# Layer 1's gate scores computed on VectorE in place of TensorE

## The chip, the cores and the metric

The kernel runs on one core of a Trainium2 chip. The metric is the device time of one execution in microseconds (us). Engines are named as in the profile: PE or TensorE (matmuls), PEld (its weight loads), DVE or VectorE, ACT or ScalarE, POOL or GpSimd, SP or SyncE, which here only issues DMAs.

## The reference

Two layers of a graph network with a gated mixture of experts behind each run on 3125 rows of 256 f32 values. The part that matters is the end of layer 1:

```python
x = x + gnn1(layernorm(x), edges)              # two mean-aggregating convolutions
n = layernorm(x)
gates = softmax(n @ gW + gb)                   # gW: 256 x 4, one column per expert
topv, topi = top_k(gates, 2)
topw = softmax(topv)
x = x + shared_mlp(n) + sum_k topw[k] * expert[topi[k]](n)
```

The change touches only how n @ gW + gb, four scores per row, is computed. Layer 0 has a gate too (8 experts); it goes through the same code with routing set and stays as it is.

## The kernel before, in words

Rows lie in 25 tiles (TILES) of 128 partitions. The function second_conv (L1780) is the second convolution of a layer, its layer norm, and the gate's scores. For layer 1 it is called with final set and routing unset; its tiles carry the tag l1b_.

TensorE first multiplies 25 dense tiles and beside them sums the neighbours of tiles 0 to 9 (early, L2284). Then one_tile (L2299) sums one tile after another, 10 to 24, with 49 matmuls each. For the work behind it, the tiles stand in seven groups, SIZES = (4, 4, 4, 4, 4, 3, 2). The table BETWEEN says at which half of which tile TensorE breaks off for a group:

```python
BETWEEN = {(12, 0): [("turn", 0)], (12, 1): [("score", 0)], (13, 0): [("back", 0)], ...
           (15, 1): [("turn", 2)], ... (18, 1): [("turn", 3)], ... (21, 1): [("turn", 4)], ...
           (24, 0): [("turn", 5), ...], (24, 1): [("score", 5), ("back", 5), ..., ("turn", 6), ...
```

- turn (L2310) waits until all tiles of the group are normalised (norm_done) and transposes them to PSUM. ScalarE copies them to SBUF (take_turned, L2207) and stores them for the final stage (xt_out).
- score (L2322) multiplies the gate's weights, padded to strips of 32 columns, with each turned tile, half of the 256 features at a time (the trace has two matmul records for each, since the data are f32). ScalarE copies the four strips (take_flat, L2219).
- back (L2335) turns the strips back into rows. VectorE adds the gate's bias and writes last_scores (take_scores, L2069).
- head: the first eight products of the final stage's experts (L1692), which run behind turns and scores of groups 5 and 6; ScalarE takes them (L1702).

VectorE works through one queue in this order: finish(0), part of finish(1) and (2), then for each group c take_scores(c) and finish(c + 2). finish adds the bias to the raw rows (L2021), adds each tile's sum from PSUM (L2027), takes the statistics (L170 to L185, with a root by ScalarE at L219) and normalises (L2045). Before it normalises over the raw rows, it waits until ScalarE's queue has stored them (x_out, L2194).

TensorE waits for VectorE in turn, and in one_tile where a bank of sums is opened again (sum_done). SyncE loads raw rows of groups 3, 4 and 5 into the place of groups 0, 1 and 2 once those are turned (load_rows, L1895), then the early weights of the final stage (final.load, L1726). The gate's weights and bias are loaded at the sixth dense tile (L1910, L1911).

The final stage, last_experts (L2981), starts when all engines have left second_conv. VectorE computes the softmax, the two largest and their weights from last_scores (from L3233); TensorE does expert products beside it, and then needs those weights for its own transposes (L3161).

Of the kernel before, what the change touches and what calls it, by code (L numbers as in the profile page):

```python
# [12 lines left out]
F32, F16, BF16, I32 = mybir.dt.float32, mybir.dt.float16, mybir.dt.bfloat16, mybir.dt.int32  # L13
ALU = mybir.AluOpType
# [4 lines left out]
P = 128  # L19
D = 256  # L20
KD = D // P
# [1714 lines left out]
SIZES = (4, 4, 4, 4, 4, 3, 2)  # L1736
STARTS = tuple(sum(SIZES[:c]) for c in range(len(SIZES) + 1))
# [3 lines left out]
STRIP = 32  # L1741
# [38 lines left out]
def second_conv(nc, io, g, adj, parts, tag, names, gate, rows_from, rows_to, work, sums_of, routing=None, final=None):  # L1780
# [4 lines left out]
    with ExitStack() as ctx:  # L1785
        pr = Prog(nc, ctx, tag, g["used_sems"])
# [3 lines left out]
        held = work.held + [third[:, :]]  # L1790
# [14 lines left out]
        normed = lambda c: labelled(c)[:, :, 0:D]  # L1805
        AFTER = {3: 0, 4: 1, 5: 2}
# [4 lines left out]
        E = gate_w.shape[1]  # L1811
        if routing:
# [14 lines left out]
            first_tile = {"xt": pr.sb("expert_xt", [P, KD, ST], F32), "xr": pr.sb("expert_xr", [P, ST // P, DW], F32),  # L1827
                          "ids_now": row_i[:, 0:2 * (ST // P)].rearrange("p (a t) -> p a t", a=2)}
            weights = expert_weights(parts, pr.sb("expert_w1", [P, KD, H0], F32), pr.sb("expert_b1", [P, 2, HB], F32))
        wg = pr.sb("gate_w", [P, KD, E], F32)  # L1830
        strips_of_wg = held[1][:, 0:KD * STRIP].rearrange("p (k e) -> p k e", k=KD)
        bg = pr.sb("gate_b", [P, E], F32)
        st = pr.sb("st", [P, CT, 6], F32)
        mv = pr.sb("mv", [P, CT, 2], F32)
# [43 lines left out]
        @block.sync  # L1878
        def _(sp):
            def load(k):  # L1880
                r = k % RING
                if k >= RING:
                    sp.wait_ge(s["dense_done"], k - RING + 1)
                for sem, count in sums_of(k):
                    sp.wait_ge(g[sem], count)
                work.load_sums(sp, k, s[f"in{r}"])
                work.load_inverse(sp, k, s[f"in{r}"])

            def load_x(k):
                if k >= XB:  # L1890
                    sp.wait_ge(s[f"pre_out{k % XB}"], 16 * (k // XB))
                sp.dma_start(xb(k), tile_of(rows_from, k)).then_inc(s[f"x_in{k % XB}"], 16)

            def load_rows(c):
                sp.dma_start(rows_of(c), chunk_of(g["pre"], c)).then_inc(s[f"rows_in{c}"], 16)  # L1895

            for u in range(XB - 1):
                sp.sem_inc(s[f"x_in{u}"], 16)
            load(LOADED)
            load_x(XB - 1)  # L1900
            for k in range(LOADED + 1, RING):
                load(k)

            def load_vectors(k):

                if k == 4:
                    sp.dma_start(by_row[:, :], g["inv"].rearrange("a (t p) -> (a p) t", p=P), allow_slow_non_contiguous=True
                                 ).then_inc(s["by_row_in"], 16)
                elif k == 5:
                    sp.dma_start(wg[:, :, :], gate_w.rearrange("(k p) e -> p k e", p=P)).then_inc(s["gate_in"], 16)  # L1910
                    sp.dma_start(bg[:, :], gate_b.rearrange("(a e) -> a e", a=1).broadcast_to([P, E])).then_inc(s["gate_in"], 16)  # L1911
                elif k == 7:
                    sp.dma_start(bias[:, :], io[b].rearrange("(a n) -> a n", a=1).broadcast_to([P, D])).then_inc(s["bias_in"], 16)

            for k in range(TILES):
                if k + RING < TILES:
                    load(k + RING)
                if 1 <= k and k + XB - 1 < TILES:
                    load_x(k + XB - 1)
                load_vectors(k)  # L1920
                if k == MOST + 2:
                    for u in range(XB):
                        sp.wait_ge(s[f"pre_out{u}"], 16 * len(range(u, MOST, XB)))
                    load_rows(0)
            for u in range(XB):
                sp.wait_ge(s[f"pre_out{u}"], 16 * uses(u))
            sp.wait_ge(s["dense_done"], TILES)
            load_rows(1)
            sp.wait_ge(s["x_out"], 16)
            for c in (2, 6):  # L1930
                load_rows(c)
            for c in (3, 4, 5):
                if routing:
                    sp.wait_ge(s[f"scattered{AFTER[c]}"], 16 * 2 * SIZES[AFTER[c]])
                sp.wait_ge(s["turned"], AFTER[c] + 1)
                load_rows(c)
            if final:


                sp.wait_ge(s["agg_done"], EARLY_TILES)  # L1940
                final.load(sp, s["final_in"])
                sp.wait_ge(s["xt_out"], 16 * 2)
                final.load_rows(sp, 0, s["final_in"])
                sp.wait_ge(s["final_in"], 16 * (final.FIRST + final.SECOND + 1))
            if routing:
                follow["sync_early"](sp)
                sp.wait_ge(s["agg_done"], TILES)
                follow["sync"](sp)
# [53 lines left out]
        def _(dve):  # L2002
# [62 lines left out]
                normalise(1)  # L2065

            def take_scores(c):
                dve.wait_ge(s["scored"], c + 1)
                nc.vector.tensor_tensor(g["scores"][:, tiles_in(c), 0:E], score_at(c),  # L2069
                                        bg[:, :].unsqueeze(1).broadcast_to([P, SIZES[c], E]), ALU.add).then_inc(s["score_done"], 1)  # L2070

            rch = Chain(dve, s["route_chain"])

# [64 lines left out]
            dve.wait_ge(s["bias_in"], 16)  # L2138
            dve.wait_ge(s["gate_in"], 32)
            dve.wait_ge(s["pre_out1"], 16 * uses(1))  # L2140
            nc.vector.memset(strips_of_wg[:, :, E:STRIP], 0.0)
            nc.vector.tensor_copy(strips_of_wg[:, :, 0:E], wg[:, :, :]).then_inc(s["gate_padded"], 1)
            if routing:
                dve.wait_ge(s["consts"], 4)
                nc.vector.tensor_copy(row_id[:, :], row_i[:, :]).then_inc(s["init"], 1)
                nc.vector.memset(pre[:, MOST, :], 0.0).then_inc(s["init"], 1)
                nc.vector.tensor_copy(down[:, :], down_i[:, :]).then_inc(s["init"], 1)
                dve.wait_ge(s["init"], 4)
                finish_early()
                for c in range(FINISHES):  # L2150
                    choose(c)
                    if c == FINISHES - 4:
                        add_bias(FINISHES - 1)
                    put(c)
                    if c + 2 < FINISHES:
                        finish(c + 2)
                nc.vector.tensor_copy(g["counts"][:, :], pre[:, SIZES[-1], :]).then_inc(s["init"], 1)
                dve.wait_ge(s["init"], 5)
                table.vector(dve)
                follow["vector"](dve)  # L2160
            else:
                dve.wait_ge(s["init"], 1)
                finish_early()
                final.constants(nc, ch)
                for c in range(FINISHES):
                    take_scores(c)
                    if c + 2 < FINISHES:
                        finish(c + 2)

        @block.scalar  # L2170
        def _(act):
# [25 lines left out]
            def take_turned(c):  # L2197
                act.wait_ge(s["turned"], c + 1)
                if c == 0:
                    for u in range(XB):  # L2200
                        act.wait_ge(s[f"pre_out{u}"], 16 * uses(u))
                else:
                    act.wait_ge(s["multiplied"], c)
                    if not routing:
                        act.wait_ge(s["xt_out"], 16 * c)
                for f in range(KD):
                    nc.scalar.activation(own[:, f, 0:SIZES[c] * P], dense_bank[f][:, 0:SIZES[c] * P], ACT.Copy  # L2207
                                         ).then_inc(s["xt_ready"], 1)
                if not routing:
                    act.wait_ge(s["xt_ready"], KD * (c + 1))  # L2210
                    act.dma_start(g["xt"][:, :, STARTS[c] * P:STARTS[c + 1] * P], own[:, :, 0:SIZES[c] * P]
                                  ).then_inc(s["xt_out"], 16)

            def take_flat(c):
                act.wait_ge(s["multiplied"], c + 1)
                if c >= 1:
                    act.wait_ge(s["scored"], c)
                strips = SIZES[c] * STRIP
                nc.scalar.activation(flat[0:strips, :], extra[0:strips, 0:P], ACT.Copy).then_inc(s["flat_ready"], 1)  # L2219
# [33 lines left out]
        def _(pe):  # L2253
# [104 lines left out]
            def between(t, half):  # L2358
                for what, c in BETWEEN.get((t, half), ()):
                    if what == "expert":  # L2360
                        if routing:
                            follow["start"](pe, c)
                        continue
                    {"turn": turn, "score": score, "back": back, "rank": rank}[what](c)
                    head(c, *HEADS_BEHIND.get((what, c), ()))

            pe.sem_inc(s["dense_done"], AHEAD)
# [1050 lines left out]
```

## Time and profile before

| What | us |
|---|---|
| Median of three runs (1176.78 to 1179.24) | 1178.76 |
| The profiled execution | 1178.69 |
| Its span, first to last instruction | 1177.2 |
| Second convolution of layer 1, from dense tiles to last head | about 852 to 1051 |
| Final stage | 1051 to 1177 |

Over the span PE is busy 1135.2 us (96%), DVE 566.1 (48%), ACT 361.8 (31%), POOL 169.1 (14%), and the mean granted TensorE clock is 0.991 of full speed. A timeline row merges consecutive operations of one line: its second number is the time from the first start to the last end. What stands in brackets is how long the engine sat idle before it and for whom. A row of a group by line has the count, the busy time in us and the mean ns of one.

### The profile page before, as it was taken

How to read it: one execution, taken by the hardware profiler on the slowest of the kernel's cores; microseconds unless marked ns; L12 is line 12 of the kernel's file. 1: busy time of each engine (PE TensorE's matmuls, PEld its weight loads, DVE VectorE, ACT ScalarE, POOL GpSimd, SP SyncE). 2: the span in 40 equal slices, each digit the busy share in tenths (PEclk: the TensorE clock that was granted, in tenths of full speed). 3: DMA queues.
4: the chain of work that ended last, by engine and by line, in shares of the span. 5: the costliest groups of instructions: out<-in, count | busy, mean ns of one | idle time of the engine just before them, and what ended most of it. 6: DMA issues, size and time to landing. Idle time of an engine off the chain costs nothing. (4 is left out here: it accounts for less than half of the span.)

```text
span 1177.2 us, 22128 instructions
## 1 busy us (share of the span) xinstructions
PE 1135.2 (96%) x8024; PEld 854.3 (73%) x8024; DVE 566.1 (48%) x1540; ACT 361.8 (31%) x697; POOL 169.1 (14%) x160
## 2 busy tenths in 40 slices
PE   5989999999999997999999899999999999999998
PEld 4667777776668886888888777555566688866765
DVE  8888888834437677211111463000044355348654
ACT  5764554422211003333333333100122201144333
POOL 3300000000000556454444300000000000001000
PEclk9999999999999998999999899999999999999999
DMA  6710000047532446466674521120065445135101
GB/s 195 212 45 13 25 25 13 26 124 179 161 107 82 144 128 181 74 122 151 112 154 71 130 90 45 67 66 32 29 182 163 127 131 162 68 91 179 45 22 42
DMA packets 134097, 118.16 MB, mean 100 GB/s; under 512 B 23030, under 2 KB 122105, under 8 KB 134016
## 3 DMA queue, kind: packets, MB, share of 16 engines
q1 hardware_dynamic: 103392, 77.67, 23.2%
q0 software_dynamic: 12448, 18.95, 8.4%
q10 hardware_dynamic: 18176, 20.45, 5.1%
q8 instruction: 52, 0.85, 0.3%
q14 instruction: 29, 0.24, 0.1%
HBM read 67.34 MB, written 49.29 MB: 99 GB/s over the span
## 5 line engine op out<-in xcount | busy, mean ns | idle before, releaser
L1372 PE MATMUL b_pa<-adj,l_parts 128*128 (+2 forms) x980 | 141.7, 296 | 0.4 <-ACT adj L1303 0.4
L1372 PEld LDWEIGHTS b_pa<-adj,l_parts 128*128 128x128 f16 x980 | 91.2, 97 | 29.5 <-issue 0.5
L1613 DVE SCALAR_TENSOR_TENSOR l_parts<-dense,scale,l_parts 128x256 f16<-128x256 f32 x48 | 23.2, 484 | 167.4 <-ACT l_parts L1604 167.4
L2748 PE MATMUL l_sum<-l_parts,ring 128*128 128x256 f32 x448 | 101.5, 380 | 0.1
L2943 POOL DMA_INDIRECT x<-ring,l_row_i x54 | 84.3, 1561 | 105.0 <-DVE ring L2890 62.6
L1580 PE MATMUL dense<-room,ring 128*128 128x512 f32 x200 | 93.9, 594 | 0.0
L2748 PEld LDWEIGHTS l_sum<-l_parts,ring 128*128 128x128 f32 x448 | 83.2, 191 | 10.3 <-issue 0.3
L2299 PE MATMUL l_sum<-l_parts,adj 128*128 128x256 f16 x735 | 82.9, 273 | 1.2 <-DVE rows L2027 1.2
L2299 PE MATMUL l1b_sum<-l_parts,adj 128*128 128x256 f16 x735 | 82.9, 273 | 0.9 <-DVE rows L2027 0.9
L2299 PEld LDWEIGHTS l_sum<-l_parts,adj 128*128 128x128 f16 x735 | 71.2, 98 | 10.7 <-issue 2.6
L2299 PEld LDWEIGHTS l1b_sum<-l_parts,adj 128*128 128x128 f16 x735 | 71.4, 98 | 10.4 <-issue 2.4
L574 DVE TENSOR_TENSOR ring<-it,key 128x1216 f16<-128x1216 f16 x75 | 59.4, 792 | 21.7 <-PE dense L1351 11.3
L2284 PEld LDWEIGHTS l1b_sum<-l_parts,adj 128*128 128x128 f16 x490 | 47.8, 98 | 20.9 <-issue 12.5
L2284 PEld LDWEIGHTS l_sum<-l_parts,adj 128*128 128x128 f16 x490 | 47.8, 98 | 20.3 <-issue 12.5
L2890 DVE TENSOR_TENSOR ring<-l_sum,l_parts 128x256 f32 (+1 forms) x54 | 22.3, 423 | 83.1 <-PE l_sum L2748 82.4
L2284 PE MATMUL l1b_sum<-l_parts,adj 128*128 128x256 f16 x490 | 57.4, 273 | 1.7 <-DVE l_parts L1613 1.1
L2284 PE MATMUL l_sum<-l_parts,adj 128*128 128x256 f16 x490 | 57.4, 273 | 1.1 <-DVEq L2130 0.6
L494 PE MATMUL n_agg<-adj,l_parts 128*128 128x512 f16 (+2 forms) x294 | 56.4, 351 | 0.0
L3110 POOL IOTA m_down_i<- 128x4 int32 x1 | 0.1, 131 | 383.9 <-POOLq L1785 383.9
L1561 ACT ACTIVATE ring<-ring 128x256 f32<-128x256 f32 (+1 forms) x50 | 20.3, 411 | 112.6 <-DVE ring L1553 95.1
L1303 ACT ACTIVATE adj<-b_pw 128x1000 f32 (+1 forms) x40 | 40.1, 1003 | 43.3 <-PE b_pw L1351 43.3
L1551 DVE SCALAR_TENSOR_TENSOR ring<-ring,unscale 128x256 f32<-128x256 f32 x50 | 24.0, 480 | 61.1 <-DMA ring<-inv 60.9
(475 smaller groups left out, 1869.9 us busy)
## 6 DMA issues: line engine op xcount, KB each, us to landing
ring<-sums_and_zt SPq DMA_DIRECT2D x50, 256.0 KB, 3.4
l_expert_xr<-slots_in SPq DMA_DIRECT2D x28, 257.0 KB, 2.8
l_parts<-in_L_ffn_W SPq DMA_DIRECT2D x12, 512.0 KB, 4.7
pre<-room ACTq DMA_DIRECT2D x34, 128.0 KB, 1.9
sums_and_zt<-ring SPq DMA_DIRECT2D x10, 320.0 KB, 2.3
ring<-inv SPq DMA_DIRECT2D x50, 64.0 KB, 4.0
sums_and_zt<-room ACTq DMA_DIRECT2D x5, 640.0 KB, 3.6
adj<-xt SPq DMA_DIRECT2D x5, 640.0 KB, 4.7
```

Source lines behind the costliest of these rows:

```text
L494: ins = nc.tensor.matmul(pairs[n % 3][f][:, 0:size], parts[:, k, a, f * P:(f + 1) * P], moving, start=start and a == 0, stop=stop and a == ...
L574: return nc.vector.tensor_tensor(out.rearrange("p r (h two) -> p r h two", two=2), names[:, 0:width].rearrange("p (h two) -> p h two", two ...
L1303: ins = nc.scalar.activation(adj[:, :, ds(group * GW * W, GW * W)].rearrange("p k (w j) -> p k w j", j=W), counts.rearrange("p w (j k) -> ...
L1372: ins = nc.tensor.matmul(pa[f][:, 0:size], parts[:, k, a, f * P:(f + 1) * P], adj[:, k, ds(r * BW, size)], start=k == 0 and a == 0, stop=k ...
L1551: ch.done(nc.vector.scalar_tensor_tensor(h, h, self.g["unscale"][:, 0:1], self.inv[:, r, :].unsqueeze(1).broadcast_to([P, KD, P]), ALU.mul ...
L1580: ins = nc.tensor.matmul(self.dense_bank[k % 2][:, :], self.h[:, k % RING, f, :], self.w[:, f, :], start=f == 0, stop=f == KD - 1)
L1613: return nc.vector.scalar_tensor_tensor(parts[:, k, 1, :], bank[:, 0:D], scale, parts[:, k, 0, :], ALU.mult, ALU.subtract)
L2284: ins = nc.tensor.matmul(acc(t), adj[:, k, t * P:(t + 1) * P], parts[:, k, a, :], start=k == 0 and a == 0 and opens(t), stop=k == LAST and ...
L2299: ins = nc.tensor.matmul(acc(t), adj[:, k, t * P:(t + 1) * P], parts[:, k, a, :], start=k == 0 and a == 0 and opens(t), stop=k == LAST and ...
L2748: ins = nc.tensor.matmul(to[t], h[:, n, t * P:(t + 1) * P], w2[:, u, n, :], start=i == 0, stop=i == HB - 1)
L2890: nc.vector.tensor_tensor(y[:, half, t, :].rearrange("p a d -> p (a d)"), products[t], b2[:, u, :], ALU.add).then_inc(s["y_done"], 1)
L2943: pool.indirect_dma_start(out=g["x1"], in_=rows, in_offset=None, compute_op=ALU.add, out_offset=bass.IndirectOffsetOnAxis(ap=at, axis=0)). ...
```

## The change

In layer 1 (no routing) the gate's weights are loaded once onto every partition as gate_rows, [128, 256, 4]: expert e's weights are every fourth value. take_scores no longer waits for TensorE. After a group is normalised, VectorE multiplies each tile's rows with gate_rows[:, :, e] and sums over the 256 features, one tensor_tensor_reduce per tile and expert, starting from the bias, straight into last_scores. Products go to two alternating buffers, each reused when the operation two before is done. TensorE's score and back and ScalarE's take_flat are left out in layer 1; turn stays, since the final stage needs the turned rows. SyncE waits for a group's scores before it loads other rows over that group. The order of VectorE's queue is as before: the scores of group c stand ahead of finish(c + 2).

```diff
-        wg = pr.sb("gate_w", [P, KD, E], F32)
-        strips_of_wg = held[1][:, 0:KD * STRIP].rearrange("p (k e) -> p k e", k=KD)
+        if routing:
+            wg = pr.sb("gate_w", [P, KD, E], F32)
+            strips_of_wg = held[1][:, 0:KD * STRIP].rearrange("p (k e) -> p k e", k=KD)
+        else:
+            gate_rows = pr.sb("gate_rows", [P, D, E], F32)
+            products = pr.sb("products", [P, 2, D], F32)
...
+                    else:
+                        sp.dma_start(gate_rows[:, :, :], gate_w.rearrange("(a d) e -> a d e", a=1).broadcast_to([P, D, E])).then_inc(s["gate_in"], 16)
...
             for c in (3, 4, 5):
                 if routing:
                     sp.wait_ge(s[f"scattered{AFTER[c]}"], 16 * 2 * SIZES[AFTER[c]])
+                else:
+                    sp.wait_ge(s["score_done"], E * STARTS[AFTER[c] + 1])
                 sp.wait_ge(s["turned"], AFTER[c] + 1)
                 load_rows(c)
...
             def take_scores(c):
-                dve.wait_ge(s["scored"], c + 1)
-                nc.vector.tensor_tensor(g["scores"][:, tiles_in(c), 0:E], score_at(c),
-                                        bg[:, :].unsqueeze(1).broadcast_to([P, SIZES[c], E]), ALU.add).then_inc(s["score_done"], 1)
+                dve.wait_ge(s["norm_done"], STARTS[c + 1])
+                for n in range(SIZES[c]):
+                    t = STARTS[c] + n
+                    for e in range(E):
+                        if E * t + e >= 2:
+                            dve.wait_ge(s["score_done"], E * t + e - 1)
+                        nc.vector.tensor_tensor_reduce(products[:, e % 2, :], normed(c)[:, n, :], gate_rows[:, :, e], 1.0, bg[:, e:e + 1],
+                                                       ALU.mult, ALU.add, g["scores"][:, t, e:e + 1]).then_inc(s["score_done"], 1)
...
             def take_turned(c):
...
-                    act.wait_ge(s["multiplied"], c)
-                    if not routing:
-                        act.wait_ge(s["xt_out"], 16 * c)
+                    act.wait_ge(s["xt_out"], 16 * c)
...
             def take_flat(c):
+                if not routing:
+                    return
...
-                    {"turn": turn, "score": score, "back": back, "rank": rank}[what](c)
+                    if routing or what == "turn":
+                        {"turn": turn, "score": score, "back": back, "rank": rank}[what](c)
```

## Rows read from the trace of the kernel before

**Rows 1.** Chain that ended last, from 940 on: start us, us, what.

```profile
1052.87 0.27 DVE l_parts L3240
...
1058.79 0.45 PE dense L3161 x5
```

**Rows 2.** Windows: stretch, its us, busy us (and instructions) per engine, PEclk, DMA share, GB/s.

```profile
972.40:1035.10 62.70, 62.70 (x615) 55.33 (x614) 25.88 (x96) 6.28 (x16) 0.00 (x0) 1.00 0.34 108
1035.10:1051.00 15.90, 14.68 (x92) 10.19 (x89) 3.84 (x17) 6.38 (x15) 0.09 (x1) 1.00 0.17 59
```

**Rows 3.** Timeline of TensorE: start us, us, engine, line, operation, out<-in, count.

```profile
984.81 1.04 PE L2310 MATMUL dense<-ident,ring 128*128 128x128 f32 x8
...
988.40 0.64 PE L2322 MATMUL l1b_extra<-room 128*32 128x128 f32 x16
...
994.33 0.27 PE L2335 MATMUL l1b_sum<-ident,room 128*128 128x128 f32 x1
994.44 8.24 PE L2299 MATMUL l1b_sum<-l_parts,adj 128*128 128x256 f16 x74
1002.52 1.04 PE L2310 MATMUL dense<-ident,rows 128*128 128x128 f32 x8
...
1020.23 1.04 PE L2310 MATMUL dense<-ident,ring 128*128 128x128 f32 x8
...
1035.21 0.82 PE L2310 MATMUL dense<-ident,ring 128*128 128x128 f32 x6
```

**Rows 4.** Timeline of VectorE, with the last take of ScalarE.

```profile
972.47 0.17 DVE L2069 TENSOR_TENSOR last_scores<-l1b_sum,l1b_gate_b 128x16 f32<-128x16 f32 x1
972.56 0.87 DVE L2027 SCALAR_TENSOR_TENSOR ring<-l1b_sum,l1b_by_row,ring 128x256 f32<-128x256 f32 x2
973.47 1.41 DVE L170 BATCH_NORM_STATS2 l1b_st<-ring 128x6 f32<-128x256 f32 x4
...
980.38 1.38 DVE L2045 TENSOR_SCALAR ring<-ring,l1b_mv,l1b_rstd 128x256 f32<-128x256 f32 x4 [2.00 <-DMA x<-ring]
...
996.47 1.22 DVE L2021 TENSOR_TENSOR ring<-ring,l1b_bias 128x1024 f32<-128x1024 f32 x1
...
1038.87 0.88 DVE L2027 SCALAR_TENSOR_TENSOR ring<-l1b_sum,l1b_by_row,ring 128x256 f32<-128x256 f32 x2 [4.64 <-PE l1b_sum L2299]
...
1042.37 0.17 DVE L180 RECIPROCAL l1b_tmp<-l1b_tmp 128x2 f32<-128x2 f32 x1 [1.35 <-ACT l1b_tmp L219]
...
1043.36 0.74 DVE L2045 TENSOR_SCALAR rows<-ring,l1b_mv,l1b_rstd 128x256 f32<-128x256 f32 x2
...
1050.03 0.53 ACT L1702 ACTIVATE l_parts<-l1b_sum,adj 128x320 f32<-128x320 f32 x1 [0.66 <-PE l1b_sum L1692]
...
1051.02 0.21 DVE L3233 COPY l_parts<-last_scores 128x100 f32<-128x100 f32 x1 [1.90 <-PEq L1785]
```

**Rows 5.** Prices: two timeline rows of ScalarE, one of VectorE, one group by line.

```profile
17.61 0.19 ACT L949 ACTIVATION_READ_ACCUMULATOR adj<-adj 128x1 f32 x1
17.83 0.20 ACT L951 ACTIVATE adj<-adj 128x2 f32<-128x2 f32 x1
...
1077.45 7.99 DVE L3264 SCALAR_TENSOR_TENSOR adj<-ring,m_weight,adj 128x256 f32<-128x256 f32 x19
...
L817 DVE TENSOR_REDUCE adj<-adj 128x5 f32<-128x1280 f32 x1 | 1.5, 1476 | 0.0
```

**Rows 6.** The stores of the raw rows (tile x, 944 to 1051), from issue to landing.

```profile
DMA to landing us min/median/max: 2.1/4.5/6.3
```

**Rows 7.** Windows at an idle TensorE in an earlier part.

```profile
664.00:666.00 2.00, 0.00 (x0) 0.00 (x0) 1.79 (x6) 0.04 (x1) 1.33 (x2) 1.00 0.40 38
...
668.00:670.00 2.00, 0.51 (x3) 0.51 (x4) 1.69 (x12) 0.67 (x2) 0.00 (x0) 0.64 0.31 45
670.00:672.00 2.00, 2.00 (x6) 1.64 (x6) 0.49 (x3) 0.38 (x1) 0.00 (x0) 0.50 0.65 158
...
674.00:676.00 2.00, 2.00 (x8) 1.65 (x7) 1.93 (x11) 0.38 (x1) 0.00 (x0) 0.65 0.39 122
```

More of the change, by code:

```diff
@@ L1909, in load_vectors @@
                 elif k == 5:
-                    sp.dma_start(wg[:, :, :], gate_w.rearrange("(k p) e -> p k e", p=P)).then_inc(s["gate_in"], 16)
+                    if routing:
+                        sp.dma_start(wg[:, :, :], gate_w.rearrange("(k p) e -> p k e", p=P)).then_inc(s["gate_in"], 16)
+                    else:
+                        sp.dma_start(gate_rows[:, :, :], gate_w.rearrange("(a d) e -> a d e", a=1).broadcast_to([P, D, E])).then_inc(s["gate_in"], 16)
                     sp.dma_start(bg[:, :], gate_b.rearrange("(a e) -> a e", a=1).broadcast_to([P, E])).then_inc(s["gate_in"], 16)
@@ L2140, in _ @@
             dve.wait_ge(s["pre_out1"], 16 * uses(1))
-            nc.vector.memset(strips_of_wg[:, :, E:STRIP], 0.0)
-            nc.vector.tensor_copy(strips_of_wg[:, :, 0:E], wg[:, :, :]).then_inc(s["gate_padded"], 1)
             if routing:
+                nc.vector.memset(strips_of_wg[:, :, E:STRIP], 0.0)
+                nc.vector.tensor_copy(strips_of_wg[:, :, 0:E], wg[:, :, :]).then_inc(s["gate_padded"], 1)
                 dve.wait_ge(s["consts"], 4)
@@ L2201, in take_turned @@
                         act.wait_ge(s[f"pre_out{u}"], 16 * uses(u))
-                else:
-                    act.wait_ge(s["multiplied"], c)
-                    if not routing:
-                        act.wait_ge(s["xt_out"], 16 * c)
+                elif routing:
+                    act.wait_ge(s["multiplied"], c)
+                else:
+                    act.wait_ge(s["xt_out"], 16 * c)
                 for f in range(KD):
```

## The prediction

> **What bounds the kernel now.** I read the chain of waits first, then the stretches, then the two engines' timelines around the change. The last part of the chain starts in the final stage: it leaves the gate arithmetic on VectorE, reaches TensorE's turning of the weights at 1058.79, and then stays on TensorE to the end [rows 1]. So a change inside layer 1's second convolution moves the end by as much as it moves the first instruction of the final stage, 1051.02 [rows 4]; what follows it takes the same 126 us. Within the convolution TensorE is full: from 972.4 to 1035.1 it is busy all of 62.7 us, VectorE 25.88 of them [rows 2]. The last stretch, 1035.1 to 1051.0, is TensorE too, with 14.68 of 15.9.
>
> The reader is to see in the timelines that the two engines hold each other. TensorE's turn of group 2 began at 984.81 and group 3's at 1002.52 [rows 3]; each needs VectorE's normalised rows, and group 2's were started at 980.38, after a wait for the DMA that stores the raw rows [rows 4]. That is some 3 us of slack (980.38 + 1.38 against 984.81). Slack of VectorE as an average is large, slack of a group's normalised rows is not.
>
> **Removed on TensorE.** Per group of four tiles: 16 records of strip matmuls, 0.64 us with a little overlap, call it 0.6, and one turn back, of which 0.11 is seen between the start of the turn and the matmul behind it (994.33 to 994.44) [rows 3]. That is 0.7 per group, 4.9 for seven groups; 1.4 of it lies before the turn of group 2, which TensorE would then reach at 984.8 - 1.4 = 983.4. From one turn to the next it needs 1002.52 - 984.81 - 0.7 = 17.0, from turn 4 to turn 5 1035.21 - 1020.23 - 0.7 = 14.3 [rows 3]. ScalarE loses its copies of the strips; it has room, I count nothing. VectorE loses seven additions of 0.17 (972.47 in [rows 4]), the small padding of the weights, and at the end its wait for the turned-back scores.
>
> **Added on VectorE.** 25 tiles x 4 experts = 100 products with a running sum, each over 128x256 f32 with both tensors in SBUF. No row of before shows one, so I bound its step d. The multiplication alone is the two-tensor row of the final stage: 19 in 7.99, 0.42 each [rows 5]. Below that, an operation that reads 256 f32 and condenses them (batch statistics) takes 1.41 / 4 = 0.35 [rows 4]. Above, a second pass for the sum: TENSOR_REDUCE takes 1.476 for 5 x 256 elements, and a tiny operation 0.17 (972.47), so (1.476 - 0.17) / 5 + 0.17 = 0.43 for 256; with the product 0.84 or so [rows 4, 5]. The sum must also be written out. ScalarE shows what that is: ACTIVATION_READ_ACCUMULATOR, after which the next instruction starts 0.22 later (17.61 to 17.83) [rows 5]. I take d = 0.42 + 0.20 = 0.62, the product at its row and the write-out near ScalarE's. The waits on the operation two before cost nothing, as the one between still runs. Both ends, 0.35 and 0.84, stay for the range.
>
> A rule of the Trainium skill bears on this: VectorE: DVE Perf Modes, section "Two Vector instructions with no wait between them", says that an operation which also writes its accumulator counts as two instructions. By it d is above 0.42 whatever the pass costs.
>
> **Where they stand, group by group.** VectorE does the 16 products of group c before the sums of group c+2, and on that hang those rows' store, their normalising and TensorE's turn. Sixteen take 9.9.
> - Group 2. The products start at 972.5, where the addition was, and end at 982.4. Then two sums 0.9, the store's landing 4.6 (median 4.5 over seven stores, 2.1 to 6.3 [rows 6]; the statistics fit beside it), four normalisations 1.4 [rows 4]: 989.3. TensorE has waited since 983.4: 5.9 lost.
> - Group 3. 9.9 + bias 1.2 + four sums 1.7 + 4.6 + 1.4 = 18.8 against TensorE's 17.0: 1008.1, 1.8 lost. Group 4 is the same: 1026.9, 1.8 lost. Its tile 19 is done some 6.5 after the turn, before VectorE asks for it.
> - Group 5 (three tiles). 9.9 + 0.9 + 1.3 + 4.6 + 1.1 = 17.8 against 14.3: 1044.7, 3.5 lost.
> - Group 6. 9.9, bias 0.7, then from the sums (1038.87) to the end of normalising (1043.36 + 0.74) 5.2, less 1.1 because ScalarE, which came 1.35 late there with head work [rows 4], is now long free: 4.1 to 4.2. Normalised at 1059.5.
> - After that come the products of groups 5 and 6 together, 20 x 0.62 = 12.4: 1071.9. Before, group 6's scores came by TensorE while it did other work, and the block ended with ScalarE's last take (1050.03 + 0.53), 0.46 ahead of 1051.02 [rows 4]. So the final stage starts at about 1072.3, 21.3 later.
>
> A check: four times 9.9 on top of VectorE's 25.88 busy is 65.5, more than the 62.7 of that stretch [rows 2], before any wait for a store.
>
> Before, from the end of the last normalising (1044.10) to ScalarE's last take (1050.56) 6.5 went by; without score and back about 5.5 are left for TensorE, against 12.8 up to the final stage: it idles some 7 us. The trace shows what that brings: TensorE has nothing from 664 to 666, and at 670 to 672 its granted clock is 0.50 of 2.4 GHz, 1.2 GHz; over the four windows from 668 to 676 (the first at 0.64, the last at 0.65, 0.50 between) 3.4 us of full-speed work are lost [rows 7]. In the final stage TensorE's first products and the gate arithmetic end close together, so I add 3. Clock lost inside the convolution falls into TensorE's waits and costs nothing.
>
> **What else moves.** The gate weights are loaded as 128 x 4 KB = 512 KB instead of 4 KB, on SyncE's queue among the loads of the dense tiles. Those are made three or four tiles ahead of their use (RING is 4), and I take 0; the other end is what a store of that size takes to land, 4.5 [rows 6]. SyncE now waits for the products of groups 0, 1, 2 before it loads the raw rows of 3, 4, 5 over them. Behind that wait stand the other two loads and the final stage's early weights and rows. Group 3's rows are asked for at 982 and needed after 999; later ones have the same distance; the last weights go out after group 2's products, near 1018 and some ten loads on, and the first head comes after tile 24, near 1048. Nothing, but if a store shares the queues with these weights it may land like the slowest, 6.3, and not 4.5.
>
> **Sum.** 21.3 + 3 = 24.3. The profiled execution took 1178.69 (span 1177.2 and 1.5 around it), as the median 1178.76. Forecast 1178.7 + 24.3 = 1203.0. While VectorE is the bound, each 0.01 of d is worth (4 x 16 + 16 + 20) x 0.01 = 1.0 us.
>
> **Rivals.**
> - *Two passes' worth, d about 0.84.* For it: two f32 tensors and a sum in one instruction, and gate_rows[:, :, e] is read with a step of 16 bytes, of which no long row of before exists. Against: the product of two SBUF tensors (0.42) costs no more than the one with a PSUM tensor (0.87 / 2) [rows 4, 5]. 22 us above the forecast: 1225. The Trainium skill has this as a rule: Advanced Engine Details and Errata, "SBUF Cachelines", asks for at least two hits on a 16-byte line for full speed, and here each element lies on its own line; Vector Engine (DVE) Microarchitecture Reference, "Points that are easy to get wrong", says that the accumulating form with two f32 sources halves its rate. No run here shows either.
> - *Faster: the product with its sum costs as little as batch statistics, d = 0.35 or below.* For it, that row; against, the two-tensor rows at 0.42 and the write-out. At d = 0.33, products 5.3: group 2 is normalised at 984.6 (1.2 lost), the later turns are not late, TensorE's saving carries through, sums of group 6 start at 1037.9 and are normalised at 1041.5; 6.6 more, and 0.4: 1048.5 against 1051.0, so 1176.2. It decides at d = 0.38: below, faster; above, the 20 products at the end outweigh TensorE's 4.9.
> - *No difference.* d between 0.34 and 0.42: at 0.42 the same steps give 1053.1, +2.1.
> - *The gate load or a slower store adds.* Up to 4.5 at the load and 1.8 for each store that lands like the slowest: inside the range.
>
> **Chances.** Forecast, d from 0.45 to 0.75: 0.50. Two passes or the step of 16 bytes: 0.37. Faster 0.04, no difference 0.05. Dearer than two passes 0.04. Range: below, d = 0.46 without loss of clock gives +5, 1184; above, 1225 and a little for the stores and the load, 1229. No change is told from a change at about 0.2% here, 2.4 us. Faster 0.04, same 0.05, slower 0.91.
>
> **What would show it.** (1) Row of the products: 100 operations, step 0.62; near 0.84 speaks for two passes. (2) TensorE's turns of groups 2 to 6 each wait for VectorE's normalised rows, 5.9 first, the sum near 13 up to turn 5 and some 6.6 at turn 6 (which came 8.9 after turn 5 before, 0.7 of it score and back). (3) No strip or back matmul in layer 1; 4.9 us less work. (4) After the last normalising, 20 products, and the final stage starts right behind them, at about 1072. (5) Granted clock at 0.50 somewhere behind 1060. (6) From the start of the final stage to the end 126 to 130 us. The forecast is wrong if the turns don't wait, if the last products end ahead of TensorE's and ScalarE's heads, or if 850 to 948 gets longer.

## The result and the profile after

The changed kernel takes 1198.28 us (median of 4 runs, 1196.57 to 1199.19); the kernel before, beside it, 1179.0 (1176.78 to 1179.89). The ratio is 1.0161, with a 95% interval of 1.0150 to 1.0173: slower, by 19 us. The forecast was 1203.0. The profiled execution is the fastest of the four, 1196.57, with a span of 1195.0.

The span grew by 17.8 us, and the traces say where. The first instruction of the final stage moved from 1051.02 [rows 4] to 1067.19, 16.2 us; from there to the end it takes 127.8 us instead of 126.2. Nothing grew ahead of the convolution: in this execution it even began 1.7 us earlier (tile 10 of the second convolution at 947.45 against 949.13).

First the row of the new work, all 100 products, and then the first two of them in the timeline of VectorE (min/median/max of one in ns; start us, us).

```profile
L2083 DVE CUSTOM_DVE_ANT_0 l1b_products<-ring,l1b_gate_rows,l1b_gate_b x60: 664/682/707, 987.1 to 1061.3; 128x256 f32<-128x256 f32 x60
L2083 DVE CUSTOM_DVE_ANT_0 l1b_products<-rows,l1b_gate_rows,l1b_gate_b x40: 660/686/707, 969.9 to 1066.0; 128x256 f32<-128x256 f32 x40
```

```profile
969.89 0.69 DVE L2083 CUSTOM_DVE_ANT_0 l1b_products<-rows,l1b_gate_rows,l1b_gate_b 128x256 f32<-128x256 f32 x1
970.50 0.09 DVE L2083 DVE_READ_ACCUMULATOR2_ANT last_scores<- 128x1 f32 x1
970.50 0.68 DVE L2083 CUSTOM_DVE_ANT_0 l1b_products<-rows,l1b_gate_rows,l1b_gate_b 128x256 f32<-128x256 f32 x1
971.11 0.08 DVE L2083 DVE_READ_ACCUMULATOR2_ANT last_scores<- 128x1 f32 x1
...
979.60 0.86 DVE L2036 SCALAR_TENSOR_TENSOR ring<-l1b_sum,l1b_by_row,ring 128x256 f32<-128x256 f32 x2
985.75 1.38 DVE L2054 TENSOR_SCALAR ring<-ring,l1b_mv,l1b_rstd 128x256 f32<-128x256 f32 x4 [1.99 <-DMA x<-ring]
...
1002.95 1.38 DVE L2054 TENSOR_SCALAR rows<-rows,l1b_mv,l1b_rstd 128x256 f32<-128x256 f32 x4
...
1023.00 1.38 DVE L2054 TENSOR_SCALAR ring<-ring,l1b_mv,l1b_rstd 128x256 f32<-128x256 f32 x4 [2.83 <-DMA x<-ring]
...
1067.19 0.21 DVE L3250 COPY l_parts<-last_scores 128x100 f32<-128x100 f32 x1 [0.49 <-PEq L1785]
```

A record lasts 0.68 us, but the next begins 0.61 after it: the step between starts is what counts. Sixteen take 969.89 to 979.60, 9.7 us, or 0.607 each. Each product is two instructions, and the read of the accumulator starts at the very instant at which the next product starts: it does not lengthen the step. Later rows show the group's normalising, of which two of the three wait for a store to land. These answer to the rows at 972.56, 980.38 and 1051.02 of [rows 4].

Now TensorE's turns, the rows that answer to [rows 3].

```profile
969.80 1.04 PE L2326 MATMUL dense<-ident,ring 128*128 128x128 f32 x8
987.19 1.97 PE L2326 MATMUL dense<-ident,ring 128*128 128x128 f32 x8 [5.66 <-DVE ring L2054]
1005.57 1.04 PE L2326 MATMUL dense<-ident,rows 128*128 128x128 f32 x8
1024.44 1.09 PE L2326 MATMUL dense<-ident,ring 128*128 128x128 f32 x8 [1.79 <-DVE ring L2054]
1040.33 0.87 PE L2326 MATMUL dense<-ident,ring 128*128 128x128 f32 x6 [1.48 <-DVE ring L2054]
1054.79 1.12 PE L2326 MATMUL dense<-ident,rows 128*128 128x128 f32 x4 [6.54 <-DVE rows L2054]
1067.43 2.40 PE L3174 MATMUL dense<-l_parts,adj 128*64 128x320 f32 x8 [5.93 <-ACTq L3202]
```

The last row is the final stage's first work on TensorE. Before, turns 2 to 5 waited for nothing [rows 3], turn 6 for 0.21 us and that first work for 1.24:

```profile
1044.15 0.66 PE L2310 MATMUL dense<-ident,rows 128*128 128x128 f32 x4 [0.21 <-DVE rows L2045]
...
1051.23 1.30 PE L3157 MATMUL dense<-l_parts,adj 128*64 128x320 f32 x8 [1.24 <-ACTq L3185]
```

Turn 3 doesn't wait after the change either. The turn of group 2 takes 1.97 us instead of 1.04: it runs behind an idle stretch at half the clock. The windows show that, and which engine is full now (columns as in [rows 2]).

```profile
970.84:1040.33 69.49, 60.57 (x538) 53.67 (x536) 62.40 (x216) 5.17 (x12) 0.00 (x0) 0.98 0.33 105
1040.33:1067.19 26.86, 14.62 (x67) 10.53 (x67) 25.78 (x89) 5.80 (x14) 0.11 (x1) 0.84 0.10 35
987.00:989.00 2.00, 1.81 (x9) 1.75 (x10) 2.00 (x8) 0.00 (x0) 0.00 (x0) 0.50 0.01 4
989.00:991.00 2.00, 2.00 (x15) 1.60 (x14) 2.00 (x7) 1.08 (x2) 0.00 (x0) 0.72 0.00 0
1062.00:1064.00 2.00, 0.00 (x0) 0.00 (x0) 2.00 (x7) 0.07 (x1) 0.00 (x0) 1.00 0.00 0
1070.00:1072.00 2.00, 2.00 (x4) 1.27 (x5) 1.66 (x11) 0.39 (x1) 0.00 (x0) 0.50 0.95 252
```

From turn 1 to turn 5 VectorE is busy 62.40 of 69.49 us (90%), where it had 25.88 of 62.7 [rows 2]; TensorE has fallen from all of it to 60.57. Behind turn 5 VectorE is busy 25.78 of 26.86. At 1062 to 1064 TensorE has nothing at all, and at 1070 to 1072, in the final stage, its granted clock is 0.50 (1.2 GHz). The bound has changed hands for the length of the convolution.

### The profile page after: what moved, and what is told of

Read it like the earlier page. It is cut to its first block and busy times, and to the rows that moved or that the text cites. A ratio compares the mean times of both kernels' runs of the same rounds, so it can differ in the third digit from the quotient of the medians.

```text
span 1195.0 us, 22087 instructions
## 1 busy us (share of the span) xinstructions
PE 1134.5 (95%) x7917; PEld 853.2 (71%) x7917; DVE 625.4 (52%) x1731; ACT 359.4 (30%) x690; POOL 168.9 (14%) x160
## 5 line engine op out<-in xcount | busy, mean ns | idle before, releaser
L2300 PEld LDWEIGHTS l1b_sum<-l_parts,adj 128*128 128x128 f16 x490 | 47.8, 98 | 20.2 <-issue 12.5
L2300 PEld LDWEIGHTS l_sum<-l_parts,adj 128*128 128x128 f16 x490 | 47.8, 98 | 20.1 <-issue 12.5
```

Of the source, the lines that this page charges most:

```text
L2300: ins = nc.tensor.matmul(acc(t), adj[:, k, t * P:(t + 1) * P], parts[:, k, a, :], start=k == 0 and a == 0 and opens(t), stop=k == LAST and ...
```

## The experiments

All were timed against the kernel before on their chip. A ratio comes from all runs of both kernels and is not quite the quotient of the two medians. "Step" is the distance between the starts of two products.

**What the step is made of.** Three kernels ask why a product takes 0.61 us. The first copies the weights once so that each expert's 256 lie side by side.

```diff
+                if c == 0 and not routing:
+                    ch.done(nc.vector.tensor_copy(gate_flat[:, :, :], gate_rows[:, :, :].rearrange("p d e -> p e d")))
...
-                        nc.vector.tensor_tensor_reduce(products[:, e % 2, :], normed(c)[:, n, :], gate_rows[:, :, e], 1.0, bg[:, e:e + 1],
+                        nc.vector.tensor_tensor_reduce(products[:, e % 2, :], normed(c)[:, n, :], gate_flat[:, e, :], 1.0, bg[:, e:e + 1],
```

> The changed kernel, with the gate weights copied once on VectorE into a tile of 4 x 256 and read without the step of 16 bytes; the copy stands in VectorE's wait for the first store. Theory (a fixed cost of the summing instruction; the step of 16 bytes is free): the step between two products stays 0.60 us, the time stays 1197 to 1200 us. Rival (the step of 16 bytes costs): the step falls to 0.42 to 0.45 us, and by 1 us per 0.01 of it, with the end of the bound by VectorE below 0.45, the time falls to 1180 to 1185. Under the rival the copy itself, 1024 elements read with that step, takes over 2 us; under the theory 0.7 to 1.3.

Measured: 1180.73 us (10 runs), ratio 1.0023 (1.0011 to 1.0036): some 16 of the 19 us are gone. In the timeline of VectorE, the copy and the first products:

```profile
951.05 1.11 DVE L2067 COPY l1b_gate_flat<-l1b_gate_rows 128x1024 f32<-128x1024 f32 x1
...
969.50 0.48 DVE L2086 CUSTOM_DVE_ANT_0 l1b_products<-rows,l1b_gate_flat,l1b_gate_b 128x256 f32<-128x256 f32 x1
969.91 0.08 DVE L2086 DVE_READ_ACCUMULATOR2_ANT last_scores<- 128x1 f32 x1
969.91 0.48 DVE L2086 CUSTOM_DVE_ANT_0 l1b_products<-rows,l1b_gate_flat,l1b_gate_b 128x256 f32<-128x256 f32 x1
970.31 0.08 DVE L2086 DVE_READ_ACCUMULATOR2_ANT last_scores<- 128x1 f32 x1
```

The step is 0.41, the price of the two-tensor row of before (0.42, [rows 5]), with the sum and its write-out included. So the write-out is free against that row, and the step of 16 bytes costs 0.20 per product, as the rival had it. The waits that are left are one of 2.0 us at turn 2, 0.3 at turn 6, and 3.8 ahead of the final stage. The copy itself reads 1024 elements at the same step in 1.11 us, 1.1 ns each, as the theory had it and not the over 2 us of the rival. What a contiguous copy of this size takes no run shows.

The second multiplies only half of the features, at the step of 16 bytes.

```diff
-                        nc.vector.tensor_tensor_reduce(products[:, e % 2, :], normed(c)[:, n, :], gate_rows[:, :, e], 1.0, bg[:, e:e + 1],
+                        nc.vector.tensor_tensor_reduce(products[:, e % 2, 0:P], normed(c)[:, n, 0:P], gate_rows[:, 0:P, e], 1.0, bg[:, e:e + 1],
```

> The changed kernel, with each product over the first 128 of the 256 features only (the scores are of half the features). The step tells price per element from fixed price. Theory (about 1.04 ns per element and 0.33 us fixed): 0.60 - 0.13 = 0.47 us, time 1184 to 1188. Rival (two cycles per element, 2.08 ns, and 0.07 us fixed): 0.60 - 0.27 = 0.33 us, time 1175 to 1178, faster than before the change.

Measured: 1175.98 us, ratio 0.9988 (0.9975 to 1.0000), the rival's time. Two products of it:

```profile
970.16 0.45 DVE L2083 CUSTOM_DVE_ANT_0 l1b_products<-rows,l1b_gate_rows,l1b_gate_b 128x128 f32<-128x128 f32 x1
...
970.54 0.45 DVE L2083 CUSTOM_DVE_ANT_0 l1b_products<-rows,l1b_gate_rows,l1b_gate_b 128x128 f32<-128x128 f32 x1
```

The step is 0.375 for 128 elements (the theory had 0.47, the rival 0.33) and 0.605 for 256: 1.8 ns per element and some 0.145 fixed. A dearer write-out would sit in the fixed part; what grew is the price per element. Contiguous, with the same fixed part, (0.406 - 0.145) / 256 = 1.0 ns per element.

The third keeps the stride and drops the sum, so that a plain product is left; the scores are set to zero once.

```diff
-                        nc.vector.tensor_tensor_reduce(products[:, e % 2, :], normed(c)[:, n, :], gate_rows[:, :, e], 1.0, bg[:, e:e + 1],
-                                                       ALU.mult, ALU.add, g["scores"][:, t, e:e + 1]).then_inc(s["score_done"], 1)
+                        nc.vector.tensor_tensor(products[:, e % 2, :], normed(c)[:, n, :], gate_rows[:, :, e], ALU.mult
+                                                ).then_inc(s["score_done"], 1)
```

> The changed kernel with a plain tensor_tensor multiplication in place of the product with its sum; weights still read with the step of 16 bytes, all waits kept (the scores are left at zero). Theory (the sum's instruction costs the extra 0.18 us): step 0.39 to 0.42 us, time 1179 to 1184. Rival (the step of 16 bytes costs it): step 0.60 or more, time as the changed kernel's, 1198.

Measured: 1189.23 us, ratio 1.0091 (1.0068 to 1.0115).

```profile
970.32 8.67 DVE L2083 TENSOR_TENSOR l1b_products<-rows,l1b_gate_rows 128x256 f32<-128x256 f32 x16
```

Sixteen in 8.67: 0.54 each, with no sum at all. Neither expectation came out: the theory had 0.39 to 0.42, the rival 0.60 or more. A contiguous operation of the same kind stands in the kernel before, an addition of two f32 tiles in SBUF. Its row, and then that of the strided product (behind the count the busy time in us and the mean ns of one):

```profile
L1553 DVE TENSOR_TENSOR ring<-ring 128x256 f32<-128x256 f32 x50 | 21.2, 425 | 1.7
L2083 DVE TENSOR_TENSOR l1b_products<-ring,l1b_gate_rows 128x256 f32<-128x256 f32 x60 | 32.3, 623 | 0.0
```

The step of 16 bytes makes a plain record 0.20 us longer (623 ns against 425). It makes the product with its sum longer by as much: 682 against 480 with contiguous weights (medians). So the stride costs 0.20 with the sum and without it. The instruction with the sum is 0.06 us longer than the plain one in either layout; SCALAR_TENSOR_TENSOR, which has no sum, lasts as long (481 ns at L3264 of the kernel before). The forecast's 0.42 was taken from that one.

These rows bear on two rules of the Trainium skill that the prediction set side by side. Advanced Engine Details and Errata, "SBUF Cachelines", wants more than one hit on a 16-byte line for full speed: the trace agrees, with 0.61 against 0.41. Vector Engine (DVE) Microarchitecture Reference, "Points that are easy to get wrong", says that the form S2S2D2_STT with two sources in SBUF that are not bf16 runs at half throughput. No run here shows that: a record of SCALAR_TENSOR_TENSOR lasts 0.48 us both with two f32 sources in SBUF (L3264) and with one of them in PSUM (L2027), and the contiguous product with its sum lasts 0.48 too. The measurement decides. Of which form the product (CUSTOM_DVE_ANT_0) is, the trace doesn't say.

**What TensorE's part is worth, and what the load costs.** One kernel leaves the products out too.

```diff
-                dve.wait_ge(s["norm_done"], STARTS[c + 1])
-                for n in range(SIZES[c]):
...
+                nc.vector.tensor_copy(g["scores"][:, tiles_in(c), 0:E], bg[:, :].unsqueeze(1).broadcast_to([P, SIZES[c], E])
+                                      ).then_inc(s["score_done"], E * SIZES[c])
```

> The changed kernel with no gate products at all: the scores are the bias, one small copy per group. What TensorE's removed strips and turns are worth by themselves. Theory (TensorE sets the pace without them): 4.9 us less work, seven times 0.7, all on the path: 1173.5 to 1175. Rival (the last group's normalising and ScalarE's takes of the heads end the stage as before): a gain of 2 us at most, 1177.

Measured: 1172.49 us, ratio 0.9952 (0.9936 to 0.9968), 5.7 us by the ratio (3.8 to 7.5). That is the whole prize of the change, if VectorE could do its part for nothing; the forecast had 4.9 for TensorE's matmuls.

Another is the kernel before with the load of 512 KB of weights added, which nothing reads.

```diff
+                        sp.dma_start(gate_rows[:, :, :], gate_w.rearrange("(a d) e -> a d e", a=1).broadcast_to([P, D, E])).then_inc(s["gate_in"], 16)
-            dve.wait_ge(s["gate_in"], 32)
+            dve.wait_ge(s["gate_in"], 32 if routing else 48)
```

> The kernel before, with the 512 KB load of the gate's weights onto all partitions added at its place and used by nothing. Theory: the loads behind it have three tiles to spare, so no change, 1178.3 to 1179.5. Rival: it delays a dense tile by its landing time, up to 4.5 us, 1182 to 1183.5.

Measured: 1178.29 us against 1179.11, ratio 0.9999 (0.9990 to 1.0008). The load costs at most 0.9 us by the interval, and nothing that these runs can tell.

**The idle time ahead of the final stage.** 52 turns of a tile that nobody reads are put behind the last head, where TensorE had nothing.

```diff
+                    if n == 7:
+                        for _ in range(52):
+                            nc.tensor.transpose(extra[:, 0:P], g["ident"][:, :], g["ident"][:, :])
```

> The changed kernel with 52 transposes of the identity into an unused PSUM bank behind the last head, so that TensorE is not idle for the 5.9 us ahead of the final stage. Theory: the final stage took 127.8 us in place of 126.2 because its first 5 us ran at a granted clock of 0.50; with the wait filled it runs at 1.00 from its start and the time falls by 1.5 to 2 us, to 1196.5. Rival: the gate arithmetic on VectorE is the later one there and hides the clock: no change.

Measured: 1196.0 us, ratio 1.0150 (1.0133 to 1.0166), not to be told from the changed kernel's. The windows of this kernel:

```profile
1064.00:1066.00 2.00, 2.00 (x20) 2.00 (x19) 2.00 (x9) 0.00 (x0) 0.00 (x0) 1.00 0.00 0
1066.00:1068.00 2.00, 2.00 (x21) 2.00 (x20) 1.91 (x8) 0.00 (x0) 0.00 (x0) 1.00 0.00 0
1070.00:1072.00 2.00, 2.00 (x12) 1.11 (x8) 1.20 (x6) 1.65 (x4) 0.00 (x0) 1.00 0.65 137
```

The clock stays at 1.00, and the final stage takes 1195.1 - 1069.31 = 125.8 us, where it took 127.8. As one profile each is thin, both kernels were run once more on one chip.

> The changed kernel itself, on the same chip as the next kernel. Expected 1196 to 1199, final stage 127.5 to 128 us, granted clock 0.50 in the first windows of it.

> The filled wait once more, beside the changed kernel on the same chip: 52 turns of a tile that nobody reads stand behind the last head on TensorE. Theory (the idle time ahead of the final stage costs clock): final stage 125.5 to 126.2 us at full granted clock, and 1.5 to 2 us less than the changed kernel beside it, less what the filling itself overruns (up to 1 us): 0.5 to 2 us less in all. Rival (the longer final stage is a difference between executions): the two have final stages of one length and the filled one is not faster.

Measured: the changed kernel 1198.12 (ratio 1.0166, 1.0151 to 1.0182), the filled one 1197.81 (1.0161, 1.0145 to 1.0176). The first ten us of the final stage, first in the changed kernel, then in the filled one:

```profile
1068.00:1078.00 10.00, 9.70 (x39) 5.35 (x40) 5.62 (x30) 6.14 (x12) 0.12 (x1) 0.83 0.61 172
```

```profile
1072.00:1082.00 10.00, 9.64 (x46) 5.34 (x47) 5.90 (x31) 6.86 (x14) 0.10 (x1) 1.00 0.60 172
```

The final stages take 127.3 (1195.4 - 1068.09) and 125.7 us (1197.8 - 1072.07). So in both pairs the stage is 1.6 to 2.0 us shorter where the wait is filled. One could object that the filled kernels only start it later. But all profiles of this document fall into the same two kinds: in nine the stage's first products took 1.30 us, and the stage took 125.7 to 126.2; in four (the changed kernel twice, contiguous weights, product only) they took 1.43 to 2.40, and it took 127.3 to 128.4. Seven of the nine have no filling. The idle time costs the stage clock, and the clock these 1.6 to 2.0 us.

The total doesn't show it. From turn 6 to the final stage the filled kernels need 13.5 us, the changed one 12.4: 1.1 is given back by the filling itself, which runs past the last product (the copy that opens the stage sat idle 1.42 us before it instead of 0.49). What is left, 0.5 to 0.9 us, is less than these runs can tell. The expected gain in time is thus neither shown nor excluded; the length of the stage and the clock are shown.

**The tail.** Groups 5 and 6 are scored by TensorE as before the change, groups 0 to 4 by the strided products.

```diff
+        K = 0 if routing else 5
+        on_vector = lambda c: c < K
...
+                if not on_vector(c):
+                    dve.wait_ge(s["scored"], c + 1 - K)
+                    nc.vector.tensor_tensor(g["scores"][:, tiles_in(c), 0:E], score_at(c),
+                                            bg[:, :].unsqueeze(1).broadcast_to([P, SIZES[c], E]), ALU.add).then_inc(s["score_done"], 1)
+                    return
```

> Groups 0 to 4 on VectorE as in the changed kernel, the last two groups (5 and 6) scored by TensorE as before the change, so no products stand behind the last normalising. Theory (the 20 products there, 12.1 us, are the end of the block): the last normalising ends at the same time, 1054.7, the final stage starts 7 to 8 us after it instead of 12.5, and TensorE has less of a wait ahead of it: 4.5 to 6.5 us less, 1192 to 1194. Rival (the late turns alone make the loss): no change within 1 us.

Measured: 1193.27 us, ratio 1.0127 (1.0111 to 1.0142), 5.0 us less than the changed kernel by the medians and 4 by the ratios. In its timeline of TensorE the waits at the turns are still there, and the final stage begins at full speed:

```profile
988.56 1.97 PE L2333 MATMUL dense<-ident,ring 128*128 128x128 f32 x8 [5.46 <-DVE ring L2054]
...
1026.71 1.97 PE L2333 MATMUL dense<-ident,ring 128*128 128x128 f32 x8 [2.20 <-DVE ring L2054]
...
1057.02 1.11 PE L2333 MATMUL dense<-ident,rows 128*128 128x128 f32 x4 [5.69 <-DVE rows L2054]
...
1065.91 1.30 PE L3181 MATMUL dense<-l_parts,adj 128*64 128x320 f32 x8 [1.24 <-ACTq L3209]
```

From turn 6 the final stage is reached 8.7 us later (1057.02 to 1065.71) where the changed kernel needs 12.4, and it takes 125.8 us where that one takes 127.8. So of the 19 us 4 to 5 belong to the 20 products at the end and the clock behind them; the other 14 to 15 are left when they are gone, with the waits at the turns.

**Both repairs.** Contiguous weights, and groups 5 and 6 by TensorE (the two diffs above together).

> Both repairs together: the weights of each expert contiguous, and the scores of groups 5 and 6 by TensorE's strips and turn as before the change; nothing is left out. In the version with contiguous weights alone the last normalising ended near 1041 and the final stage began at 1049.67, behind 20 products. Theory: VectorE has no product left behind the last normalising, so the 6.9 us that lay there before the change (1044.10 to 1051.02) come back in place of 8.7: the final stage begins near 1047.9, and as TensorE does not idle ahead of it, it runs the 126 us of before instead of 127.8. Together some 3.6 us less than with contiguous weights alone (1180.7): 1177, which is before's time within 1.5 us, 1175.5 to 1178.5; TensorE's turn 2 still waits some 2 us. Rival: the products of groups 0 to 4 bind VectorE by themselves, also contiguous, so that the extra TensorE work of groups 5 and 6 (1.4 us) adds to the waits: 1180 or above. Second rival: the granted clock in the final stage has nothing to do with the idle time; then the final stage stays at 127.8 and the time is 1179.

Measured: 1177.91 us (11 runs), ratio 0.9993 (0.9983 to 1.0002): no difference from before, within the range of the theory. Turn 2 still waits 2.1 us. From turn 2 the final stage is reached 63.9 us later (986.39 to 1050.29), against 66.5 with contiguous weights alone (983.18 to 1049.67), and it takes 125.9 us against 128.4. The stage does not begin near 1047.9, as expected, since this execution was already 3.2 us later at turn 2. The last experiment takes that wait away: group 0's scores go back to TensorE too, and only groups 1 to 4 are products. The diff is against the kernel with both repairs; the counts that the engines wait for change with it.

```diff
-        K = 0 if routing else 5
-        on_vector = lambda c: c < K
+        on_vector = lambda c: not routing and 1 <= c < 5
...
```

> Contiguous weights, and VectorE's products only for groups 1 to 4; groups 0, 5 and 6 are scored by TensorE as before the change. Nothing is left out. Theory: what remains of the wait at turn 2 (2.1 us in the version with products for groups 0 to 4) comes from group 0's products, which stand ahead of group 2's sums. Without them TensorE doesn't wait there, and its own work falls by 4 x 0.7 = 2.8 us against before, none of it given back: 1.5 to 2.8 us below before's time, 1175.5 to 1177, ratio 0.9976 to 0.9987. Rival: once TensorE gains, the products of groups 1 to 4 (6.5 us a group) make turns 3 to 5 late instead, and the time stays that of before, 1.0 within 0.0005.

Measured: 1175.79 us (7 runs) against 1178.92, ratio 0.9968 (0.9957 to 0.9979): faster than both kernels, against before by 3.1 us (3.8 by the ratio). The expectation was 1.5 to 2.8, and the profiled execution has 2.8 (1174.4 against 1177.2); what the medians have beyond that is not explained. TensorE's turns in it:

```profile
984.72 1.04 PE L2335 MATMUL dense<-ident,ring 128*128 128x128 f32 x8
1001.64 1.04 PE L2335 MATMUL dense<-ident,rows 128*128 128x128 f32 x8
1018.56 1.04 PE L2335 MATMUL dense<-ident,ring 128*128 128x128 f32 x8
1032.75 0.82 PE L2335 MATMUL dense<-ident,ring 128*128 128x128 f32 x6
1041.70 0.66 PE L2335 MATMUL dense<-ident,rows 128*128 128x128 f32 x4 [0.21 <-DVE rows L2056]
```

No turn of groups 2 to 5 waits, the turns are 16.9 apart where they were 17.7 (1002.52 to 1020.23, [rows 3]), and the final stage begins at 1048.56 instead of 1051.02. The rival (late turns 3 to 5) has nothing in the trace.

## Why the prediction was right, step by step

The forecast was +24.3 us, measured are +19.3 by the medians; direction, the way in which the engines hold each other and, within the range, size were right. What the step is made of was not, and that it came out right by value was luck. Against the profiled execution the forecast span is 1177.2 + 24.3 = 1201.5, and 1195.0 came. The 6.5 between them can be placed (positions and distances in us):

| Part | Forecast | Measured |
|---|---|---|
| Earlier start of this execution | 0 | -1.7 |
| First product, that start put right | 972.5 | 971.6 |
| First product to turn 2 | 16.8 | 17.3 |
| Turn 2 to turn 3 | 18.8 | 18.4 |
| Turn 3 to turn 4 | 18.8 | 18.9 |
| Turn 4 to turn 5 | 17.8 | 15.9 |
| Turn 5 to turn 6 | 14.8 | 14.5 |
| Turn 6 to the final stage | 12.8 | 12.4 |
| Final stage above before's 126.2 | 3 | 1.6 |

- **(1) The step, 0.62.** Measured 0.607, right by value and wrong by its composition. The forecast took 0.42 for the product and 0.20 for the write-out, by ScalarE's row. The write-out overlaps the next product and adds nothing to that 0.42; the 0.20 are the strided weights, with a sum or without one, which the forecast had put into the rival at 0.84. Two mistakes of the same size cancelled. Contiguous weights make that plain: there the forecast's law would still have given 0.62, and 0.41 was measured.
- **The law, 1.0 us per 0.01 of step.** From 0.607 to 0.406 it gives 20 us; 17.5 went by the medians, 16 by the ratios. It holds as long as VectorE binds; at 0.406 it binds at turn 2 and behind the last turn alone.
- **(2) The turns.** Waits of 5.66, 0, 1.79, 1.48 and 6.54 against 5.9, 1.8, 1.8, 3.5 and 6.6: 8.9 up to turn 5 instead of 13, and turn 3, which was to wait too, did not. The stores decide: the forecast gave each 4.6 between the last sum and the normalising, where the trace has 5.3, 3.3, 6.1 and 2.9 for groups 2 to 5 (the first from 980.49 to 985.75), a mean of 4.4. With a fast landing VectorE's own statistics are the bound, 3.3 for four tiles and 2.9 for three. Group 5 had a fast one: that is the 1.9 in the table. The landings of this block were 2.1/4.0/6.7 (min/median/max), against 2.1/4.5/6.3 [rows 6].
- **Clock inside the convolution.** "Falls into TensorE's waits and costs nothing" failed at turn 3. There is no wait there although VectorE was ready at 1002.95 + 1.38 = 1004.3: TensorE came 1.2 later, since it had run its turn 2 and what followed at 0.50 and 0.72. It cost the end nothing, since at turn 4 TensorE waits for VectorE again, 1.79 us.
- **(3) TensorE's work.** No strip or back matmul is left. The forecast's 4.9 us stand against 5.7 for the kernel without any scores.
- **(4) The tail.** Twenty products from 1054.65 to the copy at 1067.19 take 12.5 us; forecast were 12.4 and 0.4 to the start of the stage. The kernel with that tail on TensorE shows the share, 4 to 5 us.
- **(5) and (6) The clock.** 0.50 behind 1060, as forecast; the cost was 1.6 to 2.0 and not 3.
- **The load: 0.** The kernel with the load alone shows at most 0.9 us.

Of the rivals, *two passes' worth* was half right: the 16-byte step has a price, 0.20, half of the 0.42 by which that rival stood above the bare product; a half rate does not show. *No difference*, with +2.1 us at 0.42, is close to what contiguous weights gave, 2.7 at 0.41. *Faster below a step of 0.38* could not be reached by the change as written; half the features, at 0.375, lay at 0.9988, just about where that rival put its turning point.

## What to carry to other kernels

Moving work off the bounding engine pays only if the receiver has slack at each hand-over, not on average: VectorE was 41% busy before, and 16 products of 0.61 us in the path between two turns made it the bound. Where a small operand is read many times, lay it out once for the reader: a copy of 1.11 us took a third off each of 100 products. Move only the groups whose work falls into slack: here four of seven gave 0.3%, where all seven cost 1.6%.

## What the runs showed of the hardware

- A plain two-tensor f32 operation on VectorE, 128 x 256, has a record of 0.42 us with both operands contiguous and of 0.62 (a step of 0.54) with one at a step of 16 bytes. With a sum the records are 0.48 and 0.68, the steps 0.41 and 0.61. The stride costs 0.20 in both. I had expected the write-out to cost and weighed the stride as all or nothing.
- The accumulator's read (0.07 to 0.09 us) is an instruction of its own, as the Trainium skill has it (VectorE: DVE Perf Modes, "Two Vector instructions with no wait between them"), but it begins with the next product and adds nothing to the step. ScalarE's, from which I took 0.20, is no measure for it.
- TensorE's clock was granted at 0.50 after waits of 5.5 us (the turns took 1.97 instead of 1.04). Ahead of the final stage a wait of 3.8 us with contiguous weights was followed by 0.50 (first products 2.40 instead of 1.30), one of 3.1 with half the features by 1.00 (first products 1.30). Yet in the kernel with its tail on TensorE the turn at 1026.71, after a wait of only 2.2, took 1.97, while in the changed kernel the turn after 1.79 took 1.09. So the length of one wait does not tell by itself how far the clock falls; what else does is left open.
